# Finer scheduling steps in a vision tower: last attention, normalisations and additions split, and a new order of all steps

## What is computed

```python
h = _L0_tok_ref(x, ...)                            # patches and shifts, layernorm, linear
h = h + _L0_attn_ref(_layernorm(h), ...)           # attention A: 12 heads, diagonal masked but for token 0
h = h + _L0_ffn_ref(_layernorm(h), ...)            # block: ln, attention B, ln, MLP M (768 wide)
h = h + _L1_attn_ref(_layernorm(h), ...)           # attention D: over the 12 heads of a token
h = h + _L1_ffn_ref(_layernorm(h), ...)            # mixture of 32 experts, top 4 of 8 in 4 groups
```

## Time and profile before

| | us |
|---|---|
| median of 3 runs | 831.31 |
| lowest, highest | 829.63, 835.58 |
| the profiled execution: its time | 832.61 |
| its span, first to last instruction | 830.8 |
| TensorE busy | 707.0 (85%) |
| VectorE busy | 398.3 (48%) |
| GpSimd busy | 318.6 (38%) |
| ScalarE busy | 236.4 (28%) |
| mean granted clock of TensorE | 0.886 of full |

### The profile page before, as it was taken

The page is one execution under the profiler, slowest core; times in us unless marked ns, Lnnn a source line. Parts: engine busy times, 40 slices in busy tenths (PEclk is TensorE's granted clock), DMA queues, the critical chain, the costliest instruction groups (busy, mean ns, idle before and its releaser), DMA issues.

```text
span 830.8 us, 19762 instructions
## 1 busy us (share of the span) xinstructions
PE 707.0 (85%) x6364; PEld 588.6 (71%) x6364; DVE 398.3 (48%) x1167; ACT 236.4 (28%) x673; POOL 318.6 (38%) x260
## 2 busy tenths in 40 slices
PE   6956948798959998887257989999999999999995
PEld 5724635555734697675136979998999989999995
DVE  7575465634573605993982324333333333333332
ACT  3111312123234401101232333333333333333332
POOL 5722034011022420352003445655555556465654
PEclk9975958777986899796567999999999999999998
DMA  9800000000000003003012665545464565646432
GB/s 357 212 0 3 2 2 3 1 2 2 1 1 0 1 1 115 1 1 114 27 60 83 173 186 138 132 132 156 107 160 102 159 160 158 164 104 156 108 46 42
DMA packets 35046, 70.00 MB, mean 84 GB/s; under 512 B 6353, under 2 KB 21298, under 8 KB 34994
## 3 DMA queue, kind: packets, MB, share of 16 engines
q0 software_dynamic: 15840, 17.71, 12.6%
q10 hardware_dynamic: 8352, 34.30, 12.3%
q1 hardware_dynamic: 10802, 17.25, 6.3%
HBM read 59.26 MB, written 9.98 MB: 83 GB/s over the span
## 4 chain that ended last, share of the span: by engine, by line
PE 50%; DMA 19%; DVE 17%; issue 8%; POOL 2%; ACT 2%; POOLq 1%; DVEq 0%; SPq 0%
DMA arena<-normed_rows,fetch_u 13%; PE bank L1489 9%; PE bank L1481 6%; DMA out_dram<-arena,number_u 5%; PE bank L1264 4%; PE bank L1484 4%; PE bank L1338 3%; PE bank L1210 3%; PE bank L1284 2%; PE bank L1353 2%; PE bank L1377 2%; PE bank L1466 2%; PE bank L1331 2%; PE bank L1312 1%; PE bank L1302 1%
## 5 line engine op out<-in xcount | busy, mean ns | idle before, releaser
L622 POOL DMA_INDIRECT out_dram<-arena,number_u x80 | 127.0, 1588 | 36.1 <-issue 22.3
L616 POOL DMA_INDIRECT arena<-normed_rows,fetch_u x80 | 78.3, 979 | 138.7 <-DMA out_dram<-arena,number_u 54.5
L1175 DVE COPY arena<-bank 128x256 f32<-128x256 f32 x81 | 34.3, 424 | 146.7 <-PE bank L1466 140.8
L790 ACT ACTIVATE arena<-bank,arena 128x128 f32<-128x128 f32 x234 | 64.5, 375 | 119.1 <-PE bank L1484 119.1
L1489 PE MATMUL bank<-arena 128*128 128x192 f32 x468 | 82.9, 326 | 0.4 <-DVE arena L1195 0.4
L528 POOL TENSOR_SCALAR rstd<-mv 128x4 f32<-128x4 f32 x12 | 2.7, 228 | 201.0 <-DVE mv L866 201.0
L1489 PEld LDWEIGHTS bank<-arena 128*128 128x128 f32 x468 | 75.3, 190 | 0.9 <-issue 0.9
L1481 PE MATMUL bank<-arena 128*128 128x128 f32 x468 | 59.8, 278 | 0.7
L1481 PEld LDWEIGHTS bank<-arena 128*128 128x128 f32 x468 | 56.6, 191 | 4.5 <-issue 4.5
L790 ACT ACTIVATE arena<-bank,w_space 128x128 f32<-128x128 f32 x132 | 36.4, 375 | 71.6 <-PE bank L1484 71.6
L556 POOL TENSOR_TENSOR arena<-arena,v_space 128x2304 f32<-128x2304 f32 x8 | 34.5, 4317 | 55.6 <-DVE arena L1114 50.2
(11 more groups left out here) (241 smaller groups left out, 1261.9 us busy)
## 6 DMA issues: line engine op xcount, KB each, us to landing
arena<-in_moe_w_dram ACTq DMA_DIRECT2D x15, 579.0 KB, 6.2
arena<-in_moe_w_dram ACTq DMA_DIRECT2D x15, 576.0 KB, 4.5
arena<-in_xf_dram SPq DMA_DIRECT2D x8, 512.0 KB, 9.8
w_space<-in_moe_w_dram ACTq DMA_DIRECT2D x7, 579.0 KB, 5.8
w2small<-in_moe_w_dram ACTq DMA_DIRECT2D x7, 579.0 KB
w_space<-in_moe_w_dram ACTq DMA_DIRECT2D x7, 576.0 KB, 4.1
wab<-in_moe_w_dram ACTq DMA_DIRECT2D x7, 576.0 KB
arena<-in_w_dram SPq DMA_DIRECT2D x8, 480.0 KB, 9.2
```

What stands on the lines that cost most here:

```text
L616: pool.indirect_dma_start(out=mo_stage[:, s * ROWN:(s + 1) * ROWN], out_offset=None, in_=normed_rows, in_offset=bass.IndirectOffsetOnAxis( ...
L622: pool.indirect_dma_start(out=out, out_offset=bass.IndirectOffsetOnAxis(ap=number_u[:, s:s + 1], axis=0), in_=mo_res[:, s * D:(s + 1) * D] ...
L790: nc.scalar.activation(mo_hT[:, m, :], bank[2 + m][:, 0:P], ACT.Gelu, bias=b1[:, m:m + 1]).then_inc(free[2 + m], 1)
L1175: nc.vector.tensor_copy(mo_xT.rearrange("p k t -> p (k t)"), bank[1][:, 0:2 * P]).then_inc(free[1], 1)
```

## The change

The list has finer steps and another order. Nothing is computed differently, and the number and shapes of the engines' instructions stay as they were.

- `D` is replaced by five steps for each tile: `heads_in` (projections and their stores), `scores` (VectorE, and the exponential on ScalarE), `probs` (VectorE's probabilities, GpSimd's weighing), `heads_out` (TensorE's output and projection, ScalarE's store) and `heads_add` (VectorE's addition).
- `ln` keeps the statistics and GpSimd's `rstd`; the writing of the normalised tiles (and GpSimd's `add_bias` for B and M) is a step of its own, `put`. For the router, `ln` of "R" and `norm` are the two.
- `ffn` adds one tile each.
- `fc1` has an index for the branch: half 1 has six steps of three bank fills each in place of two of nine.
- The order is new.

The new list:

```diff
+        ("tok", "T", 0), ("ln", "A", 0), ("put", "A", 0), ("xT", "A", 0), ("tok", "T", 1), ("qk", "A", (0, 0)), ("ln", "A", 1), ("put", "A", 1),
+        ("qk", "A", (0, 1)), ("bias", "A", 0), ("front", "A", (0, 0)), ("front", "A", (0, 1)), ("back", "A", (0, 0)), ("xT", "A", 1),
+        ("qk", "A", (1, 0)), ("back", "A", (0, 1)), ("V", "A", 0), ("av", "A", (0, 0)), ("V", "A", 1), ("av", "A", (0, 1)), ("av", "A", (0, 2)),
+        ("av", "A", (0, 3)), ("av", "A", (0, 4)), ("qk", "A", (1, 1)), ("av", "A", (0, 5)), ("ln", "z", 0), ("put", "z", 0), ("front", "A", (1, 0)),
+        ("back", "A", (1, 0)), ("front", "A", (1, 1)), ("ln", "B", 0), ("put", "B", 0), ("back", "A", (1, 1)), ("xT", "B", 0), ("av", "A", (1, 0)),
+        ("qk", "B", (0, 0)), ("V", "B", 0), ("av", "A", (1, 1)), ("av", "A", (1, 2)), ("qk", "B", (0, 1)), ("front", "B", (0, 0)),
+        ("back", "B", (0, 0)), ("av", "A", (1, 3)), ("gumbel", "B", 0), ("front", "B", (0, 1)), ("back", "B", (0, 1)), ("av", "A", (1, 4)),
+        ("av", "B", (0, 0)), ("av", "A", (1, 5)), ("ln", "z", 1), ("av", "B", (0, 1)), ("put", "z", 1), ("ln", "B", 1), ("av", "B", (0, 2)),
+        ("put", "B", 1), ("xT", "B", 1), ("av", "B", (0, 3)), ("av", "B", (0, 4)), ("qk", "B", (1, 0)), ("qk", "B", (1, 1)), ("front", "B", (1, 0)),
+        ("av", "B", (0, 5)), ("ln", "M", 0), ("V", "B", 1), ("put", "M", 0), ("lambda", "D", 0), ("xT", "M", 0), ("back", "B", (1, 0)),
+        ("front", "B", (1, 1)), ("back", "B", (1, 1)), ("fc1", "M", (0, 0, 3)), ("fc1", "M", (0, 1, 3)), ("av", "B", (1, 0)), ("fc2", "M", 0),
+        ("ffn", "M", 0), ("fc2", "M", 1), ("ffn", "M", 1), ("fc2", "M", 2), ("av", "B", (1, 1)), ("fc2", "M", 3), ("ffn", "M", 2), ("ffn", "M", 3),
+        ("ln", "D", 0), ("av", "B", (1, 2)), ("av", "B", (1, 3)), ("put", "D", 0), ("av", "B", (1, 4)), ("av", "B", (1, 5)), ("ln", "M", 1),
+        ("xT", "D", 0), ("put", "M", 1), ("heads_in", "D", 0), ("xT", "M", 1), ("heads_in", "D", 1), ("scores", "D", 0), ("fc1", "M", (1, 0, 2)),
+        ("heads_in", "D", 2), ("fc1", "M", (1, 0, 1)), ("fc1", "M", (1, 0, 0)), ("probs", "D", 0), ("scores", "D", 1), ("probs", "D", 1),
+        ("heads_out", "D", 0), ("heads_in", "D", 3), ("fc1", "M", (1, 1, 2)), ("heads_add", "D", 0), ("fc1", "M", (1, 1, 1)), ("fc1", "M", (1, 1, 0)),
+        ("heads_out", "D", 1), ("fc2", "M", 4), ("scores", "D", 2), ("probs", "D", 2), ("fc2", "M", 5), ("scores", "D", 3), ("fc2", "M", 6),
+        ("ffn", "M", 4), ("ffn", "M", 5), ("ffn", "M", 6), ("fc2", "M", 7), ("heads_out", "D", 2), ("probs", "D", 3), ("ffn", "M", 7), ("ln", "D", 1),
+        ("put", "D", 1), ("xT", "D", 1), ("heads_in", "D", 4), ("heads_add", "D", 1), ("heads_add", "D", 2), ("scores", "D", 4),
+        ("heads_out", "D", 3), ("heads_in", "D", 5), ("heads_in", "D", 6), ("probs", "D", 4), ("heads_add", "D", 3), ("ln", "R", 0),
+        ("scores", "D", 5), ("heads_in", "D", 7), ("norm", "R", 0), ("scores", "D", 6), ("probs", "D", 5), ("heads_out", "D", 4), ("scores", "D", 7),
+        ("heads_out", "D", 5), ("probs", "D", 6), ("heads_add", "D", 4), ("heads_out", "D", 6), ("probs", "D", 7), ("heads_add", "D", 5),
+        ("gates", "R", 0), ("heads_out", "D", 7), ("begin", "R", 0), ("heads_add", "D", 6), ("heads_add", "D", 7), ("ln", "R", 1), ("norm", "R", 1),
+        ("gates", "R", 1), ("slots", "R", 0), ("slots", "R", 1), ("counts", "R", 0), ("begin", "R", 1), ("table", "R", 0),
+                half, part, i = n
+                for m in range(3 * part, 3 * part + 3):
+                    use(m % 3, "fc1", i, m)
```

The core of the code that goes with it:

```diff
-            def ln_stats(src, t0, t1):
+            def ln_stats(L, n):
...
                 ins.then_inc(sem("ln_stats"), 1)
-                ln[0] += 1
-                dve.wait_ge(sem("ln_rstd"), ln[0])
+                ln[L, n] = len(ln) + 1
...
             def layernorm(L, n):
                 src, dst = STREAMS[L]
...
+                dve.wait_ge(sem("ln_rstd"), ln[L, n])
                 for t in range(4 * n, 4 * n + 4):
...
-            def add_ffn(n):
-                for t in range(4 * n, 4 * n + 5):
...
+            def add_ffn(t):
+                dve.wait_ge(sem("biased_M"), t + 1)
+                ps = filled(dve, "fc2", t)
+                tt(out=z[:, t, :], in0=ps[:, 0:D], in1=z[:, t, :], op=ALU.add).then_inc(free_of("fc2", t), 1)
+                was_read(dve, "fc2", t)
+                link(tt(out=h[:, t, :], in0=z[:, t, :], in1=h[:, t, :], op=ALU.add))
...
-            def attend_heads(n, s):
+            def head_exps(t):
+                act.wait_ge(sem("D_shifted"), t + 1)
+                nc.scalar.activation(scD[t % 3], scD[t % 3], ACT.Exp, scale=(HD // 2) ** -0.5).then_inc(sem("D_exp"), 1)
+
+            def store_heads(q):
+                ps = filled(act, "D", "oT", q)
...
-                elif step_name == "D":
-                    attend_heads(*n)
+                elif step_name == "scores":
+                    head_scores(n)
+                elif step_name == "probs":
+                    head_probs(n)
+                elif step_name == "heads_add":
+                    add_heads(n)
```

More of the change, by code:

```diff
@@ L352, in plan @@
             elif step == "fc1":
-                half, part = n
-                for i in (3,) if half == 0 else (2, 1, 0):
-                    for m in range(3 * part, 3 * part + 3):
-                        use(m % 3, "fc1", i, m)
+                half, part, i = n
+                for m in range(3 * part, 3 * part + 3):
+                    use(m % 3, "fc1", i, m)
             elif step == "fc2":
                 use(n % 3, "fc2", n)
-            elif step == "D":
-                half, s = n
-                for t in projected(half, s):
-                    use(4 + t % 2, L, "qk", t)
-                    use(6, L, "V", t)
-                if 0 <= s - 2 < 4:
-                    use(7, L, "oT", 4 * half + s - 2)
-                    use(3, L, "proj", 4 * half + s - 2)
+            elif step == "heads_in":
+                use(4 + n % 2, L, "qk", n)
+                use(6, L, "V", n)
+            elif step == "heads_out":
+                use(7, L, "oT", n)
+                use(3, L, "proj", n)
             elif step == "norm":
@@ L568, in _ @@
                 elif step_name == "ln":
-                    ln_rstd(4 * n, 4 * n + 4)
-                    if L in "BM":
-                        add_bias(L, n)
+                    ln_rstd(L, n)
+                elif step_name == "put" and L in "BM":
+                    add_bias(L, n)
                 elif step_name == "V" and L == "A":
@@ L715, in widen_bias, with hidden @@
                     nc.scalar.activation(value_bias[:, k, :], ones[0:HC, :], ACT.Copy, scale=cols_sb[:, c + k:c + k + 1]).then_inc(sem("bias_wide"), 1)
-            def hidden(n, part):
-                for i in (3,) if n == 0 else (2, 1, 0):
-                    for m in range(3 * part, 3 * part + 3):
-                        ps = filled(act, "fc1", i, m)
-                        nc.scalar.activation(hT[i][:, m, :], ps[:, :], ACT.Gelu, bias=b1_sb[:, m:m + 1]).then_inc(free_of("fc1", i, m), 1)
+            def hidden(n, part, i):
+                for m in range(3 * part, 3 * part + 3):
+                    ps = filled(act, "fc1", i, m)
+                    nc.scalar.activation(hT[i][:, m, :], ps[:, :], ACT.Gelu, bias=b1_sb[:, m:m + 1]).then_inc(free_of("fc1", i, m), 1)
             def store_qv(t):
@@ L1123, in _ @@
                 elif step_name == "ln":
+                    ln_stats(L, n)
+                elif step_name == "put":
                     layernorm(L, n)
@@ L1327, in hidden @@
                     loaded(pe, "mlp")
[L1328 to L1338 removed]
+                p0, p1, ks = ((0, HC, (1,)), (KEEP[2], KEEP[1], (0,)), (0, KEEP[2], (0,)), (0, HC, (0, 1)))[i]
+                for m in range(3 * part, 3 * part + 3):
+                    ps = claim("fc1", i, m)
+                    for k in ks:
+                        ins = mm(ps[:, :], w1[p0:p1, k, m * P:(m + 1) * P], xT[p0:p1, k, n * HALF:(n + 1) * HALF], start=(i >= 2 and k == 0), stop=(k == ks[-1]), skip_group_check=(i < 2))
+                    ins.then_inc(full_of("fc1", i, m), 1)
             def ffn_out(t):
@@ new lines, in heads_in, with heads_out @@
+                    ins.then_inc(full_of("D", name, t), 1)
+            def heads_out(q):
+                pe.wait_ge(sem("D_weighed"), q + 1)
+                ps = claim("D", "oT", q)
+                for k in range(2):
+                    for b in range(H):
+                        c = b * D + k * HC
+                        ins = mm(ps[0:HC, k * P:(k + 1) * P], prodV[q % 2][:, c:c + HC], ident[:], start=(b == 0), stop=(b == H - 1))
+                ins.then_inc(full_of("D", "oT", q), 1)
+                was_read(pe, "D", "oT", q)
+                ps = claim("D", "proj", q)
+                for k in range(2):
+                    ins = mm(ps[:, 0:D], oT_heads[:, q % 2, k, :], wout["D"][:, k, :], start=(k == 0), stop=(k == 1))
```

(1 more changed line is left out.)

182 lines of the change are left out of this document (67 added, 115 removed), and 17 rows, old and new, of the table NEG.

## The result

| | before | changed |
|---|---|---|
| median, us (4 runs each) | 833.44 | 809.12 |
| lowest, highest | 829.63, 836.14 | 805.94, 809.80 |
| the profiled execution, its span | 832.61, 830.8 | 805.94, 804.2 |

The ratio is 0.9738, 95% interval 0.97 to 0.9777: faster. In a second set of runs it was 0.9769 (0.9737 to 0.9802; 811.81 against 831.72). The forecast of 813 us was 0.978 of the median before it.

A forecast was written before the change was run, and what follows sets the result against it. Only the tower behind the expert loop could move, bound by engines waiting for each other: -1 - 6 - 2 - 1 - 9 - 3 = -22, 4 taken back, 814.6 for the profiled execution, so a median of 813 us; range 801 to 826.

The forecast's parts named there:

- Stage 1: Start to the transposes of B half 0: 1 us less, with z half 0 normalised during A half 1's scores.
- Stage 2: On to the transposes of B half 1: 6 us less by earlier spreading and filled waits, 1.5 us taken back for clock.
- Stages 3 and 4: To fc2's first tile, 2 us less; then to D's first scores, 1 us less.
- Stage 5: MLP half 1 with D half 0, 80.9 us: 12.9 or 5.4 us less by fc1's pace, 9 taken.
- The three lost places: Stage 5's old losses: TensorE's 6.1 us for `xT` M, slow first nine fills (15.85 us), VectorE's 12.3 us before tile 2.
- The port lock: `ffn` 7's second addition may wait up to 1.8 us for GpSimd's weighing; output 2 covers it to about 0.5 us.
- Stage 6: D half 1 to the end of `gates`: 3 us less, with scores 5 filling the wait for `rstd`; VectorE is the bound.
- Behind it, nothing: From `heads_add` 6 on, each engine keeps its old order, a chain of 55 us: no gain.
- The 4 us taken back for hand-overs: Allowance over the whole sum for some hundred hand-overs between engines: 4 us, an estimate.
- the one of more gain: Rival: TensorE gets the upper clock level through stages 2 and 5; 800 to 806 us, chance 0.15.
- The one of returning waits: Rival: waits come back elsewhere, such as VectorE's 10 us before probs 2; 820 to 829 us, chance 0.2.
- The slower one: Rival: fc1 in threes with table loads between keeps TensorE at the lower level in stage 5; 840 and above, chance 0.05.

The follow-up runs named there:

- e1: Changed kernel with its finer steps put back in the old order; 837.66 us against 838.68 us for the kernel before, ratio 0.9977.
- e10: Changed kernel with `put` directly behind its `ln` for z and B half 1, D half 0 and the router's half 0; 822.59 us, 0.9799 of the kernel before.
- e11: Changed kernel with tiles 2 and 3 of A's half 1 behind both score blocks of B's half 0; 824.01 us, 0.9837 of the kernel before.
- e0: The changed kernel run again, unaltered, as measure for three later runs on one chip; 811.81 us, 0.9769 of the kernel before.
- e8: Changed kernel with `begin` R 0 moved behind `norm` R 1; 806.98 us, 0.9715 of the kernel before.
- e4: Changed kernel's order up to the transposes of D half 1, old order behind; 823.39 us, 0.9811 of the kernel before.
- e7: Changed kernel with `ffn` 7, `ln` D 1 and `put` D 1 ahead of `probs` 3, `heads_add` 1 ahead of `scores` 3; 804.63 us, 0.969 of the kernel before.
- e3: Changed kernel with the old order up to D's first scores, new order behind; 829.44 us, 0.9904 of the kernel before.
- e9: Changed kernel with both the `ffn` 7/`heads_add` 1 move of e7 and the `begin` move of e8; 804.15 us, 0.9662 of the kernel before.
- e5: Changed kernel with `xT` M of half 1 put back behind `scores` 0 of D; 826.45 us, 0.9886 of the kernel before.
- e6: Changed kernel with the projections of D's tiles 1 and 2 behind the first nine fills of fc1; 822.28 us, 0.9823 of the kernel before.
- e2: Changed kernel's order up to D's first scores, old order behind; 826.44 us, 0.9834 of the kernel before.

## Why the prediction was right, step by step

**That only the tower moves, and that order moves it:** right. The loop's length varies, but not with the order (392 to 397 us in five orders, 400 to 407 in eight others); e1 gave no gain with the finer steps alone.

**Stage 1 (-1):** too small. The new order has 76.7 to 80.4 us in its executions, the old one 80.4, 82.2 and 81.7: about -3. The 0.8 us that I charged for the bias of A behind `qk` A (0,1) doesn't show in the difference. No run undoes a part of this stage, so its cause within the stage stays open.

**Stage 2 (-6):** the profiled execution had -3.8, others of the same order -5.8 (45.4) and -6.3 (44.9). The step that was off is "the second block then ends at 146.2, and B's first tile is spread at 150.7", 33.0 us into the stage: it was 37.1 and 34.5. A projection of B's queries takes 3.60 us at the full level. The new order puts the first one right behind the transposes, which follow an idle of 5.7 us (in both executions), and there it took 6.52 us in the one execution (clock 0.55) and 5.48 in the other (0.66):

```profile
119.12 6.52 PE L1256 MATMUL bank<-xT,wab 96*96 96x512 f32 x8
```
```profile
120.11 5.48 PE L1256 MATMUL bank<-xT,wab 96*96 96x512 f32 x8
```

The chain behind the first tile, forecast at 10.9 us, took 10.3 (152.49 to 162.81), with both waits for `rstd` filled. So the 1.5 us that I took back for the clock is a term whose size isn't fixed. Without it the forecast length of the stage is 43.9 us, and one and the same program took 44.9 and 47.4: 1.0 and 3.5 us.

**Stages 3 and 4 (-2, -1):** -1.5 and -1.2. Right. But e10 and e11 show what the second hides: the changed kernel keeps the full clock through stage 4 (1.00, before 0.93), and two orders with changes ahead of it, e10 and e11, lose 2.9 us to the clock there.

**Stage 5 (-12.9 or -5.4, -9 taken):** -11.5 in the profiled execution, -8.3 in e0 and -8.2 in e8. The two ends that I had computed, the pace of either batch, were the right question. With this order in place the first batch took 10.1 us in seven profiles (e0, e4, e7 to e10 and the changed kernel's), but 12.9 in e3 and 12.7 in e11, which differ from them only ahead of the stage; the second took 8.38 us in the changed kernel's and in e9's alone, else 10.1 to 11.7. The difference between the executions of the changed kernel is one row. Here is e0's, for the 8.38 us of the changed kernel's profiled execution:

```profile
252.48 11.73 PE L1324 MATMUL bank<-xT,w_space 64*128 64x512 f32 x18
```

The program, the instruction before it and its length are the same. The three lost places are gone as named. e5 says that giving the first back costs 12 us. e6 says that giving the third back costs 7, but on TensorE's own path and not through VectorE's wait, so my sentence that VectorE's idle time sets no end isn't refuted. What I called a wait of 6.1 us was a wait and a clock.

**The port lock (0.5 us at one place of the prediction, 1.3 at another, in the sum nowhere):** the mechanism was right, the cover wrong. The addition was held 1.9 us, and with `heads_add` 1 behind it 1.7 us of that were on the path. I had taken output 2's matmuls as cover and not thought of its projection, which hung on VectorE.

**Stage 6 (-3):** -2.5, and right in its mechanism; like for like it is more. The old order takes 58.6 us in the kernel before, e1 and e2. The new one takes 56.0 to 56.5 in the changed kernel, e0, e5, e6, e8 and e11, where the first projection ran at the lower level (3.8 to 4.2 us), and 54.6 in e3, e7 and e9, where it ran at the full one (2.18), as it did before: -4.0. **"Behind it, nothing":** -1.1 in the routing of the profiled execution, +0.4 in e0's. Right within what executions differ.

**The 4 us taken back for hand-overs:** nothing in the runs shows such a loss. Without them the sum is -22; e0 and the changed kernel measured -19.9 and -24.3 by medians. No run shows the term. In e0's profile each of the six stages lies within 0.7 us of its forecast with nothing taken back. In the first profile stage 1 gave 1.7 us more than forecast, stage 2 gave 2.2 less and stage 5 gave 2.5 more than the middle that I took, so there the sum is near in part by luck.

**The rivals:** the one of more gain came in part: stage 5 ran at 0.95 and brought 11.5 us, but stage 2 fell to 0.64 in the same execution. The one of returning waits named the 10 us before `probs` 2, which came (11.3); TensorE ran fc2 without idle time meanwhile, so it cost nothing. The slower one (fc1 in threes keeps TensorE at the lower level) was the opposite of what happened: fc1 went from 26.9 us to 18.5 and, in e0, 21.8.

## What to carry to other kernels

Price a stall of TensorE in a small-matmul stage as the wait plus what the next instructions may lose at the lower clock level: here giving back one wait of 5.3 us cost 12. A number that comes near isn't the mechanism: in e6 the stage grew as the theory said, and the row of output 0's store shows that it wasn't by the theory's path. When a step is moved, list its instructions on every queue: the gain on TensorE in e8 was given back on ScalarE.
